# A two-layer graph network on one core: new order lists in a written-out program, maxima with turned sign, GpSimd's long instructions by graph

## The chip, the core and the metric

One core of one Trainium2 chip. The metric is the device time of one execution of the program in microseconds (us); lower is better. The engines are TensorE (PE; its weight loads are PEld), VectorE (DVE), ScalarE (ACT), GpSimd (POOL) and SyncE (SP), which here only issues DMAs. Each runs its own instruction stream, and they are ordered by semaphores alone.

## The reference

128 graphs of 128 nodes with 256 features, and an adjacency matrix each.

- **Layer 0** is a transformer block: layer norm; q, k, v (8 heads of 32); scores with `0.1 * adj` added where there is an edge and minus infinity elsewhere; softmax; product with v; output projection `wo` and residual; layer norm; `w1` (256 to 1024), gelu, `w2` (1024 to 256), residual.
- **Layer 1** has two rounds (C0 and C1 below), each: `q = x Wq + bq`, `k = x Wk + bk` (128 wide), scores divided by sqrt(128), masked softmax, `ctx = attn x`, `ctx Wc`, `x = layernorm(x + ctx) * g + b`.

```python
attn = jax.nn.softmax(scores, axis=-1)
x1 = residual + (out @ wo + bo)
mlp = jax.nn.gelu(n2 @ w1 + b1, approximate=False) @ w2 + b2
...
ctx = jnp.einsum('boi,bid->bod', attn, x)
ctx = jnp.einsum('bnd,ed->bne', ctx, Wc[k])
x = layer_norm(x + ctx, ln_g[k], ln_b[k])
```

## The kernel before, in words

**Tiling.** Four graphs form a group (NG = 32 groups). A group's rows are held as [128 nodes, 4 graphs, 256 features], its transposes as [128 features, 2 halves, 512 nodes]. f32 products are made of f16 parts: every operand is a high part (a cast, on ACT) and a low part (the rest, on DVE or POOL), and `mm3` (L243 to L247) issues high x high, high x low, low x high. So nearly each result of PE is read twice out of PSUM, by ACT for the high part and by DVE for the low part.

**Stages of a group.** `N`: load x (SP), statistics (DVE, L574 and L579), reciprocal root (POOL, `rsqrt`, L404 and L406), normalize (DVE `xh`, L587), transpose (PE `N.xT`), and `xb` adds the output bias on POOL (L441). `Q`: q0, q1, k0, k1 (halves of q and k; ACT L479, DVE L666), v0, v1. `stk`: SP copies q and k into the layout of the heads, 12 DMAs (L348). `A`, per graph b: `S` scores (PE L1041; DVE adds the mask, L680), `max` (DVE L685, and L687 turns the sign and scales into `nbias`), `exp` (ACT L490, one instruction a head), `PT` transposes (PE L1048; ACT L496, DVE L691), `AV` (PE; DVE L695, L699); then `oT`, `wo` (DVE L711), `st`, `xh`, and `x1b` on POOL (L437). `M`: `mT` (DVE L720), eight blocks `up` (PE, then gelu and cast on ACT, L510 and L513), `lo` (the low part, L252; even blocks DVE, odd ones POOL) and `down`; `x2` (DVE L728). `C0`, `C1`: `xT`, `q`, `k` (ACT L525), `S` (PE L1102, DVE L741), `max` (DVE L744, and L746 turns the sign of four numbers a partition), `ex` (ACT L532), `xW` (ACT L540), `cWb` (POOL L427, C1 only), `PT` (PE L1113, ACT L544), `PV` (PE L1122, DVE L763), `st`, `rs`, `xh`, and `af` (POOL L414 and L416: gain, then bias); `sto` stores the output.

**Order.** Five lists, one for each engine, give the steps of one iteration (`TENSOR`, `SCALAR`, `VECTOR`, `GPSIMD`, `SYNC`). The number behind a step says which group it treats: in iteration n, `A.S2-1` is the score step of graph 2 of group n - 1. So an iteration has every stage once, of groups n + 1 to n - 4. `run` (L266) writes out the first and last iterations and runs the rest in a hardware loop, two iterations to a turn; here PE's iterations -1 to 7 and 30 to 35 are written out and 8 to 29 looped. The waits are made by `need` (L222): "this semaphore has reached the count of group g"; in the loop the count is worked out in a register.

**What waits for what.** PSUM has eight banks: 0 and 1 for A (`psA`), 2 for q, k, v and AV, 3 for q, k, v and `up` (`psUp`), 4 and 5 for M, 6 and 7 for C and N. A step of PE can start when its operands are there and the last reader of its bank is done: PE's `Q.k1` waits for DVE's q1 (same bank), `C1.PT` for ACT's eviction of C1.xW, `up0` for DVE's low part of mT. `hid_h` and `hid_l` are rings of three blocks. `adj_in` is one buffer that both masks use (`mA` for A, `mC` for C). SP's list is in order too: a load whose wait isn't over holds back the store behind it. `C0.af` on POOL waits until the last output left `x3` (`st_out`).

## Time and profile before

| | |
|---|---|
| time of the runs | 2272.46 us, median of 3 (2272.21 to 2272.55) |
| profiled execution | time 2277.72 us, span 2275.9 us |
| busy share of the span | PE 89%, DVE 83%, ACT 69%, PEld 66%, POOL 37% |
| PE's granted clock | 0.970 of full over the span |
| DMA | 108.6 MB, mean 48 GB/s |

The span goes from the first to the last instruction of the profiled execution; the time has 1.8 us around it. A busy PE counts overlapping matmuls, so its pitch is read from where matmuls start. Iterations are told by PE's list: iteration 4 starts at 247.6 us, 8 at 505.4, 30 at 1946.8 and 32 at 2079.5.

### The profile page before, as it was taken

How to read it: one execution, taken by the hardware profiler on the slowest of the kernel's cores; microseconds unless marked ns; L12 is line 12 of the kernel's file. 1: busy time of each engine (PE TensorE's matmuls, PEld its weight loads, DVE VectorE, ACT ScalarE, POOL GpSimd, SP SyncE). 2: the span in 40 equal slices, each digit the busy share in tenths (PEclk: the TensorE clock that was granted, in tenths of full speed). 3: DMA queues.
4: the chain of work that ended last, by engine and by line, in shares of the span. 5: the costliest groups of instructions: out<-in, count | busy, mean ns of one | idle time of the engine just before them, and what ended most of it. 6: DMA issues, size and time to landing. Idle time of an engine off the chain costs nothing.

```text
span 2275.9 us, 47439 instructions
## 1 busy us (share of the span) xinstructions
PE 2026.2 (89%) x16984; PEld 1512.2 (66%) x16984; DVE 1887.3 (83%) x3589; ACT 1562.6 (69%) x2994; POOL 845.8 (37%) x632
## 2 busy tenths in 40 slices
...
DMA packets 103649, 108.61 MB, mean 48 GB/s; under 512 B 9824, under 2 KB 78432, under 8 KB 103456
## 3 DMA queue, kind: packets, MB, share of 16 engines
...
q0 software_dynamic: 544, 0.80, 0.2%
...
## 4 chain that ended last, share of the span: by engine, by line
PE 56%; DVE 21%; ACT 13%; issue 7%; POOL 1%; DMA 0%; SPq 0%; DVEq 0%; POOLq 0%; ACTq 0%
PE ps L245 13%; PE ps L247 13%; PE ps L246 13%; PE ps L824 5%; PE ps L1122 5%; PE ps L1048 3%; DVE hid_l L252 3%; DVE nmax L685 3%; ACT area L490 3%; DVE xh L587 2%; PE ps L1102 2%; DVE rot_l L720 2%; DVE qk L666 2%; DVE st L574 1%; ACT L490 1%
## 5 line engine op out<-in xcount | busy, mean ns | idle before, releaser
L252 POOL TENSOR_TENSOR hid_l<-area,hid_h 128x512 f16<-128x512 f32 x128 | 148.7, 1162 | 748.7 <-ACT hid_h L513 748.7
L490 ACT ACTIVATE area<-area,nbias 128x128 f32<-128x128 f32 x1024 | 313.5, 392 | 1.0 <-DVE nbias L687 0.2
L245 PE MATMUL ps<-w_h,hid_h 128*128 128x256 f16 x1024 | 279.0, 272 | 2.7 <-DVE hid_l L252 1.6
L247 PE MATMUL ps<-w_h,hid_l 128*128 128x256 f16 x1024 | 279.1, 273 | 0.0
L246 PE MATMUL ps<-w_l,hid_h 128*128 128x256 f16 x1024 | 279.1, 273 | 0.0
L510 ACT ACTIVATE area<-ps,b_col 128x512 f32<-128x512 f32 x256 | 176.1, 688 | 83.5 <-PE ps L247 82.4
L680 DVE TENSOR_TENSOR area<-ps,biasA 128x1024 f32<-128x1024 f32 x128 | 155.6, 1216 | 66.1 <-PE ps L1041 66.0
L245 PE MATMUL ps<-rot_h,w_h 128*128 128x512 f16 x512 | 195.0, 381 | 12.7 <-DVE rot_l L720 11.2
L246 PE MATMUL ps<-rot_l,w_h 128*128 128x512 f16 x512 | 194.7, 380 | 0.0
L247 PE MATMUL ps<-rot_h,w_l 128*128 128x512 f16 x512 | 194.7, 380 | 0.0
L404 POOL TENSOR_TENSOR ve<-mv,eps_cols 128x4 f32<-128x4 f32 x128 | 26.7, 209 | 418.4 <-DVE mv L579 417.5
L525 ACT ACTIVATE cq<-ps,cb_col 128x512 f32<-128x512 f32 x64 | 43.9, 686 | 192.1 <-PE ps L247 192.1
L245 PE MATMUL ps<-xT_h,wqk_h 128*128 128x512 f16 x256 | 100.0, 390 | 76.6 <-DVE qk L666 51.5
L513 ACT CAST hid_h<-area 128x512 f16<-128x512 f32 x256 | 158.3, 618 | 8.2
L691 DVE TENSOR_TENSOR pT<-ps,pT 128x1024 f16<-128x1024 f32 x128 | 155.3, 1214 | 5.4 <-ACT pT L496 5.4
L685 DVE TENSOR_REDUCE nmax<-area 128x8 f32<-128x1024 f32 x128 | 155.3, 1213 | 1.1
L824 PE MATMUL ps<-ident,area 128*128 128x128 f32 x1024 | 136.7, 277 | 21.9 <-DVE area L587 19.1
L252 DVE TENSOR_TENSOR hid_l<-area,hid_h 128x512 f16<-128x512 f32 x128 | 137.7, 1076 | 21.7 <-ACT hid_h L513 20.5
L416 POOL TENSOR_TENSOR x<-x,cb_row 128x1024 f32<-128x1024 f32 x64 | 153.7, 2401 | 5.0
L427 POOL TENSOR_TENSOR area<-area,cwb_row 128x1024 f32<-128x1024 f32 x32 | 75.3, 2352 | 199.8 <-ACT area L540 199.8
L1048 PE MATMUL ps<-ident,area 128*128 128x128 f32 x1024 | 138.5, 280 | 11.3 <-ACT area L490 7.0
L245 PE MATMUL ps<-cw_h,cT_h 128*128 128x256 f16 x512 | 141.0, 275 | 6.1 <-DVE cs L741 6.1
...
## 6 DMA issues: line engine op xcount, KB each, us to landing
...
area<-in_L_gnn_w SPq DMA_DIRECT2D x2, 1024.0 KB, 11.6
area<-in_L_gnn_Wc SPq DMA_DIRECT2D x2, 256.0 KB, 11.6
...
```

What stands on the lines that cost most here:

```text
L245: pe.matmul(dst, lh, rh, start=start, stop=False, **kw)
L246: pe.matmul(dst, lh, rl, start=False, stop=False, **kw)
L247: return pe.matmul(dst, ll, rh, start=False, stop=stop, **kw)
L252: eng.tensor_tensor(hid_l[:, c % RING, :], hidden[:, c % 2, :], hid_h[:, c % RING, :], ALU.subtract).then_inc(done, 1)
L490: last = act.activation(sc[:, b % 2, h], sc[:, b % 2, h], ACT.Exp, bias=nbias[:, b, h:h + 1], scale=1.0 / QK_SCALE)
L510: act.activation(hidden[:, b % 2, :], psUp, ACT.Gelu, bias=b1_col[:, b:b + 1], scale=1.0 / W_SCALE).then_inc(a_gelu, 1)
L513: act.copy(hid_h[:, b % RING, :], hidden[:, b % 2, :]).then_inc(a_hi, 1)
L680: dve.tensor_tensor(sc[:, b % 2], psA_heads, biasA[:, b].unsqueeze(1).broadcast_to([P, H, P]), ALU.add).then_inc(d_S, 1)
L685: dve.tensor_reduce(nmax[:, b, :], sc[:, b % 2], AX.X, ALU.max).then_inc(d_max, 1)
L691: dve.tensor_tensor(pT16[:, b % 2, 1], psA_heads, pT16[:, b % 2, 0], ALU.subtract)\
L824: last = pe.transpose(dst[:, c, b * P:(b + 1) * P], rows[:, b, c * P:(c + 1) * P], ident[:, :])
L1048: last = pe.transpose(psA_heads[:, h], sc[:, b % 2, h], ident[:, :])
```

## The change

- The five lists have a new order, and the program is written out: no loop, all waits on constants. PE's waits for free PSUM banks (`freed`, in place of the branches of `need`) name the last reader of the bank by group.
- `tensor_reduce(..., negate=True)` gives minus the maximum. The two instructions that turned the sign (L687, L746) go. The scale 1/QK_SCALE moves from `exp` and `nbias` into the scores' step (scalar_tensor_tensor in place of tensor_tensor, L680), and the factor 1024 of the probabilities from the exponent into the two evictions of `PT` (L496, L691).
- POOL's seven long instructions of an iteration (L414, L416 twice each, L427, L437, L441; 128x1024) become four each, one for each graph (128x256), with the semaphore on the last.
- The ring of feed-forward blocks has four places.

```diff
-P_SCALE = math.log(1024.0)
-RING = 3
+P_SCALE = 1024.0
+RING = 4
...
-TENSOR = ["Q.k0+0", "M.down2-2", "A.S2-1", "M.up4-2", "C0.q-3", "A.PT1-1", "M.down3-2", "M.up5-2",
-          "C0.k-3", "Q.q0+0", "M.up6-2", "C0.S-3", "M.down4-2", "A.S3-1", "C0.xW-3", "Q.q1+0",
-          "A.AV0-1", "A.PT2-1", "M.down5-2", "A.AV1-1", "Q.k1+0", "C0.PT-3", "A.PT3-1", "A.AV2-1",
-          "C1.xT-4", "M.up7-2", "A.AV3-1", "M.down6-2", "A.oT-1", "C0.PV-3", "M.down7-2", "A.wo-1",
-          "C1.q-4", "C1.k-4", "A.S0+0", "C1.S-4", "Q.v1+0", "C1.xW-4", "M.mT-1", "A.S1+0",
-          "C1.PT-4", "Q.v0+0", "M.up0-1", "C1.PV-4", "A.PT0+0", "M.up1-1", "N.xT+1", "M.down0-1",
-          "M.up2-1", "M.down1-1", "C0.xT-2", "M.up3-1"]
-SCALAR = ["C0.xT-3", "M.up3-2", "A.exp1-1", "M.up4-2", "C0.q-3", "Q.k0+0", "M.up5-2", "C0.k-3",
-          "A.PT1-1", "Q.q0+0", "M.up6-2", "A.exp2-1", "C0.ex-3", "Q.q1+0", "C0.xW-3", "A.PT2-1",
-          "A.exp3-1", "Q.k1+0", "C0.PT-3", "A.PT3-1", "C1.xT-4", "M.up7-2", "A.oT-1", "C1.q-4",
-          "C1.k-4", "Q.v1+0", "C1.ex-4", "C1.xW-4", "M.mT-1", "C1.PT-4", "A.exp0+0", "M.up0-1",
-          "Q.v0+0", "M.up1-1", "A.PT0+0", "N.xT+1", "M.up2-1"]
-VECTOR = ["A.PT1-1", "C0.S-3", "C0.max-3", "Q.q0+0", "A.S3-1", "A.max3-1", "A.AV0-1", "M.lo6-2",
-          "Q.q1+0", "A.PT2-1", "A.AV1-1", "Q.k1+0", "A.AV2-1", "A.PT3-1", "C1.xT-4", "A.AV3-1",
-          "Q.mA+0", "A.oT-1", "C0.PV-3", "M.x2-2", "A.wo-1", "A.st-1", "A.S0+0", "C1.S-4",
-          "C1.max-4", "A.xh-1", "A.max0+0", "N.st+1", "Q.v1+0", "M.mT-1", "A.S1+0", "N.xh+1",
-          "C1.PV-4", "M.lo0-1", "A.max1+0", "Q.v0+0", "M.mC-2", "N.xT+1", "A.PT0+0", "M.lo2-1",
-          "C1.st-4", "C0.xT-2", "A.S2+0", "C0.st-3", "C1.xh-4", "M.lo4-1", "Q.k0+1", "C0.xh-3",
-          "A.max2+0"]
-GPSIMD = ["M.lo1-1", "M.lo3-1", "N.xb+1", "C1.rs-4", "C0.rs-3", "M.lo5-1", "C1.af-4", "A.x1b-1",
-          "C0.af-3", "M.lo7-1", "A.rs+0", "C1.cWb-3", "N.rs+2"]
-SYNC = ["Q.ldA+0", "Q.stk+0", "N.ld+1", "M.ldC-2", "C1.sto-4"]
+TENSOR = ["A.S2-1", "M.up3-2", "M.down1-2", "C0.xT-3", "M.up4-2", "M.down3-2", "Q.k0+0", "A.PT1-1",
+          "M.down2-2", "M.up5-2", "C0.q-3", "Q.q0+0", "M.up6-2", "C0.k-3", "A.S3-1", "Q.q1+0",
+          "C0.S-3", "A.AV0-1", "M.down5-2", "A.PT2-1", "C0.xW-3", "M.down6-2", "Q.k1+0", "C0.PT-3",
+          "A.AV1-1", "A.PT3-1", "A.AV2-1", "C1.xT-4", "M.up7-2", "A.AV3-1", "M.down4-2", "A.oT-1",
+          "C0.PV-3", "M.down7-2", "A.wo-1", "C1.k-4", "C1.q-4", "A.S0+0", "C1.S-4", "Q.v1+0",
+          "C1.xW-4", "M.mT-1", "Q.v0+0", "A.S1+0", "C1.PT-4", "M.up0-1", "A.PT0+0", "C1.PV-4",
+          "M.up1-1", "M.down0-1", "M.up2-1", "N.xT+1"]
+SCALAR = ["A.exp1-1", "C0.xT-3", "M.up4-2", "Q.k0+0", "A.PT1-1", "M.up5-2", "C0.q-3", "Q.q0+0",
+          "M.up6-2", "C0.k-3", "A.exp2-1", "Q.q1+0", "C0.ex-3", "A.PT2-1", "C0.xW-3", "A.exp3-1",
+          "C0.PT-3", "Q.k1+0", "A.PT3-1", "C1.xT-4", "M.up7-2", "A.oT-1", "C1.k-4", "C1.q-4",
+          "Q.v1+0", "C1.ex-4", "M.mT-1", "C1.xW-4", "A.exp0+0", "C1.PT-4", "M.up0-1", "A.PT0+0",
+          "M.up1-1", "M.up2-1", "N.xT+1", "Q.v0+0", "M.up3-1"]
+VECTOR = ["Q.k1+0", "A.AV2-1", "A.PT3-1", "A.AV3-1", "C1.xT-4", "A.oT-1", "C0.PV-3", "M.x2-2",
+          "A.wo-1", "A.st-1", "A.S0+0", "C1.S-4", "C1.max-4", "A.xh-1", "A.max0+0", "N.st+1",
+          "Q.v1+0", "M.mT-1", "A.S1+0", "M.mC-2", "N.xh+1", "A.max1+0", "M.lo0-1", "C1.PV-4",
+          "A.PT0+0", "C1.st-4", "N.xT+1", "Q.v0+0", "C1.xh-4", "M.lo2-1", "A.S2+0", "C0.xT-2",
+          "A.max2+0", "Q.k0+1", "C0.st-3", "M.lo4-1", "A.PT1+0", "Q.q0+1", "A.S3+0", "C0.S-2",
+          "A.max3+0", "C0.max-2", "A.AV0+0", "M.lo6-1", "Q.q1+1", "Q.mA+1", "A.PT2+0", "C0.xh-3",
+          "A.AV1+0"]
+GPSIMD = ["M.lo7-2", "A.rs-1", "N.rs+1", "C1.cWb-4", "M.lo1-1", "C1.rs-4", "M.lo3-1", "C1.af-4",
+          "N.xb+1", "M.lo5-1", "A.x1b-1", "C0.rs-3", "C0.af-3"]
+SYNC = ["Q.stk-2", "N.ld-1", "Q.ldA-1", "M.ldC-3", "C1.sto-6"]
...
-            start, stop = (4 - min(aheads)) // 2, (NG - max(aheads)) // 2
-            for n in range(-max(aheads), 2 * start):
-                iteration(n // 2, n % 2)
-            with eng.Fori(start, stop) as it:
-                iteration(it, 0)
-                iteration(it, 1)
-            for n in range(2 * stop, NG - min(aheads)):
+            for n in range(-max(aheads), NG - min(aheads)):
                 iteration(n // 2, n % 2)
...
-            def over_graphs(row):
-                return row.unsqueeze(1).broadcast_to([P, B, D])
+            def by_graph(dst, src, row, op, signal):
+
+                for b in range(B):
+                    last = pool.tensor_tensor(dst[:, b], src[:, b], row, op)
+                last.then_inc(signal, 1)
 
             def affine(g, l, dst, src):
 
                 need(pool, d_xh[2 + l], g, 1, 1)
-                pool.tensor_tensor(dst, src, over_graphs(cg_row[:, l, :]), ALU.mult).then_inc(p_cg[l], 1)
+                by_graph(dst, src, cg_row[:, l, :], ALU.mult, p_cg[l])
                 need(pool, p_cg[l], g, 1, 1)
-                pool.tensor_tensor(dst, dst, over_graphs(cb_row[:, l, :]), ALU.add).then_inc(p_c[l], 1)
+                by_graph(dst, dst, cb_row[:, l, :], ALU.add, p_c[l])
...
-                                                  bias=nbias[:, b, h:h + 1], scale=1.0 / QK_SCALE)
+                                                  bias=nmax[:, b, h:h + 1])
...
-                        act.copy(pT16[:, b % 2, 0], psA_heads).then_inc(a_PT, 1)
+                        act.activation(pT16[:, b % 2, 0], psA_heads, ACT.Copy, scale=P_SCALE).then_inc(a_PT, 1)
...
-                        dve.tensor_tensor(sc[:, b % 2], psA_heads,
-                                          biasA[:, b].unsqueeze(1).broadcast_to([P, H, P]),
-                                          ALU.add).then_inc(d_S, 1)
+                        dve.scalar_tensor_tensor(sc[:, b % 2], psA_heads, 1.0 / QK_SCALE,
+                                                 biasA[:, b].unsqueeze(1).broadcast_to([P, H, P]),
+                                                 ALU.mult, ALU.add).then_inc(d_S, 1)
                     elif stage == "A" and what[:3] == "max":
                         need(dve, d_S, g, B, b + 1)
-                        dve.tensor_reduce(nmax[:, b, :], sc[:, b % 2], AX.X, ALU.max).then_inc(d_max, 1)
-                        need(dve, d_max, g, B, b + 1)
-                        dve.tensor_scalar(nbias[:, b, :], nmax[:, b, :], -1.0 / QK_SCALE, P_SCALE,
-                                          ALU.mult, ALU.add).then_inc(d_nb, 1)
+                        dve.tensor_reduce(nmax[:, b, :], sc[:, b % 2], AX.X, ALU.max, negate=True).then_inc(d_max, 1)
                     elif stage == "A" and what[:2] == "PT":
                         need(dve, a_PT, g, B, b + 1)
-                        dve.tensor_tensor(pT16[:, b % 2, 1], psA_heads, pT16[:, b % 2, 0], ALU.subtract)\
-                           .then_inc(d_PT, 1)
+                        dve.scalar_tensor_tensor(pT16[:, b % 2, 1], psA_heads, P_SCALE, pT16[:, b % 2, 0],
+                                                 ALU.mult, ALU.subtract).then_inc(d_PT, 1)
...
-                            dve.tensor_reduce(cneg[:, l], cs[:, l], AX.X, ALU.max).then_inc(d_cmax[l], 1)
-                            need(dve, d_cmax[l], g, 1, 1)
-                            dve.tensor_scalar(cmax[:, l], cneg[:, l], -1.0, None, ALU.mult).then_inc(d_cnb[l], 1)
+                            dve.tensor_reduce(cmax[:, l], cs[:, l], AX.X, ALU.max, negate=True).then_inc(d_cmax[l], 1)
...
+            def freed(g, *before):
+
+                pair, odd = g
+                for signal, behind, per, k in before:
+                    if not isinstance(pair, int):
+                        pe.wait_ge(signal, pair * (2 * per) + ((odd - behind) * per + k))
+                        return
+                    group = 2 * pair + odd - behind
+                    if 0 <= group < NG:
+                        pe.wait_ge(signal, group * per + k)
+                        return
+
...
-                    elif step == "C1.S":
-                        need(pe, a_cq[1], g, 1, 1)
-                        if isinstance(it, int):
-                            need(pe, d_cy[0], g, 1, 2)
-                            need(pe, d_xT, g, 1, 5)
...
+                    elif step == "C1.S":
+                        freed(g, (a_cq[1], 0, 1, 1))
...
```

The other branches of `freed` follow the same pattern.

## Rows read from the trace of the kernel before

**Rows 1.** The page, busy time, share of the span and instructions of each engine.

```profile
PE 2026.2 (89%) x16984; PEld 1512.2 (66%) x16984; DVE 1887.3 (83%) x3589; ACT 1562.6 (69%) x2994; POOL 845.8 (37%) x632
```

**Rows 2.** Windows: stretch and length, busy PE, PEld, DVE, ACT, POOL, PE clock, DMA.

```profile
0.00:247.60 247.60, 174.53 (x1353) 126.53 (x1354) 155.28 (x287) 127.86 (x237) 44.39 (x55) 0.88 0.24 65
247.60:505.40 257.80, 245.10 (x2114) 184.49 (x2113) 233.82 (x435) 193.98 (x372) 98.08 (x72) 1.00 0.18 47
505.40:1946.80 1441.40, 1352.43 (x11617) 1018.39 (x11616) 1284.83 (x2443) 1066.28 (x2046) 574.71 (x418) 1.00 0.19 49
...
2079.50:2276.00 196.50, 129.37 (x857) 89.70 (x855) 97.41 (x217) 78.24 (x154) 77.70 (x51) 0.85 0.05 17
```

**Rows 3.** Timeline of PE, 477 to 495 us: start, us, what [idle before].

```profile
477.74 0.27 PE L245 MATMUL ps<-wo_h,rot_h 128*128 128x256 f16 x1
...
480.36 0.38 PE L245 MATMUL ps<-cT_h,cqk_h 128*128 128x512 f16 x1
...
493.22 0.38 PE L245 MATMUL ps<-rot_h,w_h 128*128 128x512 f16 x1 [0.28 <-DVE rot_l L720]
...
494.51 0.81 PE L1122 MATMUL ps<-area,cs 128*128 128x256 f32 x3
```

**Rows 4.** Pieces of the critical chain: start us, us, what.

```profile
469.26 0.02 PE ps L245
...
469.83 0.03 PE ps L247
...
1017.71 1.73 PE ps L1122 x8
1019.44 0.87 PE ps L1048 x8
...
1044.37 0.89 PE ps L1102 x8
...
1046.57 0.45 PE ps L1041 x8
```

**Rows 5.** PE's waits (us, times, longest): 247.6 to 505.4 twice, 505.4 to 1946.8 once.

```profile
PE ps L245 <- DVE qk L666: 6.6, 4, 2.3
PE ps L1113 <- ACT area L540: 2.4, 4, 0.6
...
PE ps L245 <- issue: 19.4, 10, 2.2
```

**Rows 6.** Timelines of DVE and POOL, 450 to 481 us.

```profile
457.21 2.36 POOL L437 TENSOR_TENSOR area<-area,b_row 128x1024 f32<-128x1024 f32 x1
...
457.33 2.26 DVE L746 TENSOR_SCALAR cmax<-cneg 128x4 f32<-128x4 f32 x1
...
462.86 2.36 POOL L416 TENSOR_TENSOR x<-x,cb_row 128x1024 f32<-128x1024 f32 x1
...
463.32 2.44 DVE L252 TENSOR_TENSOR hid_l<-area,hid_h 128x512 f16<-128x512 f32 x1
...
480.89 1.23 DVE L711 SCALAR_TENSOR_TENSOR area<-ps,xin 128x1024 f32<-128x1024 f32 x1
```

**Rows 7.** Groups by line: shapes, count | busy us, mean ns | idle before.

```profile
L746 DVE TENSOR_SCALAR cmax<-cneg 128x4 f32<-128x4 f32 x64 | 60.1, 939 | 2.2
L687 DVE TENSOR_SCALAR nbias<-nmax 128x8 f32<-128x8 f32 x128 | 45.0, 351 | 4.4
L680 DVE TENSOR_TENSOR area<-ps,biasA 128x1024 f32<-128x1024 f32 x128 | 155.6, 1216 | 66.1 <-PE ps L1041 66.0
...
L441 POOL TENSOR_TENSOR xin<-xin,bo_row 128x1024 f32<-128x1024 f32 x32 | 75.3, 2355 | 3.3 <-DVE area L587 3.3
...
L404 POOL TENSOR_TENSOR ve<-mv,eps_cols 128x4 f32<-128x4 f32 x128 | 26.7, 209 | 418.4 <-DVE mv L579 417.5
```

**Rows 8.** The instructions of L746: shortest/median/longest ns, first and last start.

```profile
L746 DVE TENSOR_SCALAR cmax<-cneg x64: 169/171/2264, 202.7 to 2251.9; 128x4 f32<-128x4 f32 x64
```

**Rows 9.** Timeline of SP's DMA queue, the 12 copies of one group.

```profile
469.56 9.19 SPq L348 DMA_DIRECT2D qkS<-qk  x12
```

More of the change, by code:

```diff
@@ L153, in graph_blocks @@
         nmax = sb("nmax", [P, B, H])
-        nbias = sb("nbias", [P, B, H])
         rec = sb("rec", [P, B, H])
@@ L426, in iteration @@
                         need(pool, a_cW[1], g, 1, 1)
-                        pool.tensor_tensor(cW, cW, over_graphs(cwb_row[:, :]), ALU.add)\
-                            .then_inc(p_cW, 1)
+                        by_graph(cW, cW, cwb_row[:, :], ALU.add, p_cW)
                     elif stage == "C0" and what == "af":
@@ new lines, in iteration @@
+                    if step == "A.S2":
+                        freed(g, (d_PT, 0, 4, 1))
+                    elif step == "M.up3":
+                        freed(g, (a_gelu, 0, 8, 3))
+                    elif step == "C0.xT":
+                        freed(g, (d_xT, -3, 1, 1), (d_cy[1], 2, 1, 1), (d_cy[0], 1,
+                              1, 1))
+                    elif step == "M.up4":
+                        freed(g, (a_gelu, 0, 8, 4))
+                    elif step == "Q.k0":
+                        freed(g, (d_v[0], 1, 1, 1))
+                    elif step == "A.PT1":
+                        freed(g, (d_S, 0, 4, 3))
+                    elif step == "M.up5":
+                        freed(g, (a_gelu, 0, 8, 5))
+                    elif step == "C0.q":
+                        freed(g, (d_cT[0], 0, 1, 1))
+                    elif step == "Q.q0":
+                        freed(g, (d_qk[2], 0, 1, 1))
+                    elif step == "M.up6":
+                        freed(g, (a_gelu, 0, 8, 6))
+                    elif step == "C0.k":
+                        freed(g, (d_cT[0], 0, 1, 1))
+                    elif step == "A.S3":
+                        freed(g, (d_PT, 0, 4, 2))
+                    elif step == "Q.q1":
+                        freed(g, (a_gelu, 2, 8, 7), (d_v[1], 1, 1, 1))
+                    elif step == "C0.S":
+                        freed(g, (a_cq[0], 0, 1, 1))
+                    elif step == "A.AV0":
+                        freed(g, (d_qk[0], -1, 1, 1), (d_v[0], 0, 1, 1))
+                    elif step == "A.PT2":
+                        freed(g, (d_S, 0, 4, 4))
+                    elif step == "C0.xW":
+                        freed(g, (d_cS[0], 0, 1, 1))
+                        freed(g, (a_ck[0], 0, 1, 1))
+                    elif step == "Q.k1":
+                        freed(g, (d_qk[1], 0, 1, 1))
+                    elif step == "C0.PT":
+                        freed(g, (a_cW[0], 0, 1, 1))
+                    elif step == "A.AV1":
+                        freed(g, (d_o, 0, 4, 1))
```

198 lines of the change are left out of this document (43 added, 155 removed).

## The prediction

> **What bounds the kernel now.** I read the page first: TensorE (PE) is busy 89% of the span and VectorE (DVE) 83%, so either may set the time, and the shares don't say which [rows 1]. The stretches come next. Iterations 4 to 7 of the order list (each brings one group of four graphs through every stage) take 257.8 us, 64.5 each; iterations 8 to 29 take 1441.4 us, 65.5 each [rows 2]. The first four are written out already, the others run in the hardware loop. Written out alone is thus worth at most about a microsecond an iteration; the level of 65 has another cause.
>
> What PE must do in an iteration follows from counts in the code and the pitch at which its matmuls start at full clock [rows 3, 4]. Six matmuls of 512 columns take 1.29 us: 96 of them 20.7. The 24 of wo (256 columns) take 2.62: 192 of them 21.0. Eight transposes take 0.87: 80 of them 8.7. Eight score matmuls 0.45, four times: 1.8. C's f32 scores 0.89 and its last product 1.73, twice each: 5.2. 96 small AV matmuls, 23 of them in 0.57: 2.4. The sum is **59.8 us**. So some 4.7 to 5.7 us of every iteration is PE waiting, and the waits say for whom [rows 3, 5]:
> - 1.7 us on average and up to 2.3 before Q.k1, for DVE's q1 (it frees the PSUM bank).
> - 12.86 us pass between the end of wo (480.36) and the start of up0 (493.22), where PE has 10.9 us of work: 1.9 us are lost, 0.6 of them for C1.xW's eviction (C1.PT) and the last ones for DVE's mT (up0).
> - The rest, 0.7 us in the written stretch, is crumbs of 0.1 to 0.3 at S3, AV0 and PT2, and in the loop the jump back (below).
>
> Why is DVE late? Not by its arithmetic. The maximum's sign turn in C0.max, four numbers a partition, took 2.26 us, and GpSimd's (POOL) x1b was running from 457.21 to 459.57; DVE's lo6 (normally 0.68) took 2.44, until POOL's add of 2.36 was over [rows 6]. Over the run these sign turns take 0.94 us on average and 0.17 in the median, the nbias ones, as small, 0.35 on average [rows 7, 8]. DVE instructions with SBUF operands only are held until POOL's current instruction ends. So q1 stands behind lo6 behind a 2.36 us POOL instruction, and PE behind q1. That is what ends the longest wait.
>
> **The change, part by part.**
> (1) *Sign turned in the reduction.* Four nbias and two cmax instructions an iteration go. Without a hold each costs 0.17 and two semaphore hops: the reduction's end to the next start is 0.03 + 0.17 - 0.08 = 0.12, and becomes -0.08, so 0.2 saved each, 1.2 for six. With the holds in their means it is 6 x 0.2 + 4 x (0.35 - 0.17) + 2 x (0.94 - 0.17) = 3.5 us of DVE per iteration. That negating costs the reduction anything is not in the trace; bounds: nothing, or a second small instruction of 0.17 inside (which only gives back the 1.2). I take nothing. The scale moves into scalar_tensor_tensor instead of tensor_tensor; at 128x1024 from PSUM the one took 1.23 (L711), the other 1.22 [rows 6, 7], so eight of them cost under 0.1. The copy with a scale on ACT I take at the plain cast's price.
> (2) *POOL by graph.* Seven instructions of 2.36 an iteration become 28. A piece of 128x256 lies between a quarter, 0.59, and the line through 128x4 (0.209) and 128x1024 (2.355), 0.74 [rows 7]. I take 0.65: 2.6 instead of 2.36 a step, POOL stays under half busy. A hold on DVE is then at most 0.7 instead of 2.4. Whether DVE gets in between two pieces with no wait between them is not shown. In the trace it got in at the next boundary even where POOL's next instruction started at once, so I take that it does. If it does not, the long holds stay.
>  The Trainium skill says the same lock otherwise (SBUF — State Buffer, SBUF: two separate sides): the shared port pair goes to whoever starts first, for the whole instruction. By that rule too pieces shorten the hold. Its GPSIMD Engine Reference (3.1) speaks against pieces, since each instruction pays a software dispatch again; by the 0.74 bound, which has such a cost in it, this makes an af pair 5.9 instead of 4.7 us.
> (3) *Written out.* In the loop PE waits 19.4 us for nothing that the profile shows, ten times up to 2.2, at the list's end [rows 5]. This goes. The written stretch shows no new wait in its place. It is contained in the per-iteration sum below, since that starts from the floor.
> (4) *Order.* Q.k0 moves behind up3, down1, C0.xT, up4, down3; Q.q1 on DVE stands well before PE's Q.k1: PE reaches k1 25.9 us into its list, DVE can finish q1 at about 24. The wait of 1.7 to 2.2 us goes. Late next is Q.k1's own way: on ACT it stands behind exp3 and C0.PT, DVE ends it about 30.0 into the list. Behind it SP issues 12 copies in 9.2 us [rows 9], landed 2.3 later: 41.5, and S0 needs them at 42.9. Covered with 1.4 us. In SP's list the adjacency load for C waits for mA, which now ends late, and the store of the output is queued behind it; POOL's C0.af waits for that store. DVE has seven instructions (6.3 us) and some waits before C0.PV needs that af (5.2 us in pieces plus about 1 for the store). Covered, with 2 us.
>  Now the stretch wo to up0, zero at wo's end. DVE's order there is the old one, and each step takes its pitch in the timeline of before: wo to 1.4, st 3.4, S0 4.5, C1.S 5.1, C1.max 5.8, xh 7.1, max0 8.3, N.st 10.1, v1 10.7, mT 11.85, PE's up0 at **12.0** (before 12.86: 0.4 less by two removed instructions, 0.4 because DVE's wo started only at 480.89, behind x2 [rows 6]). ACT's side gives the same: mT is transposed at 9.3, ACT mT to 10.5, C1.xW to 11.5, C1.PT 11.6, up0 12.1. Against 10.9 that is a stall of 1.1. Then exp0 (11.5 to 13.95 on ACT) must precede PT0, which stands right behind up0 (13.4) instead of behind C1.PV: 0.7 us of new stall. C1.PV needs POOL's cWb, now queued behind N.rs: 0 to 0.5, I take 0.1. PT2 behind exp2 and other crumbs: 0.1 to 0.4, I take 0.2. Ring of four: up4 and later need a down less, which only gives cover; nothing.
>  Sum: 59.8 + 1.1 + 0.7 + 0.1 + 0.2 = **61.9 us** an iteration, bounds 60.4 (stretch well covered) and 63.5 (pieces at 0.74 and every crumb of before kept).
>
> **The sum**, against the profiled execution (span 2275.9, time 2277.7, median of the runs 5.3 lower). Iterations 4 to 31 stand between 247.6 and 2079.5 [rows 2]: 1831.9 us. 28 x 61.9 = 1733.2. Filling (247.6) and draining (196.4) are chains of one group with PE at 0.88 and 0.85 of its clock; fewer DVE steps give back a few us, POOL's pieces cost some: -6, between -15 and +8. Span 2275.9 - 98.7 - 6 = 2171.2; plus 1.8 outside, less 5.3: **2167.7**, say 2167.
>
> **Rivals.**
> - *PE at its floor* (60.5 or less). For it: DVE is busy 58.5 us an iteration (233.8 over four [rows 2]) and 3.5 of it go, and by my walk PE waits for it at wo to up0 alone. Against: exp0 before PT0. 28 x 60.4 with -6: 2126.
> - *The holds stay.* POOL's pieces are back to back, DVE doesn't get in, or each piece is dear; only the removed instructions and the order help. Half of the 5.1 us of waiting is kept, 63.5 to 65: 2212 to 2250.
> - *Slower, by C0.af.* Eight pieces in place of two, behind a store that is issued later, with 7.5 us or so until C0.PV(next) writes over their input and PE waits behind DVE. It costs nothing up to 0.9 us a piece; from there 8 us per us of piece. From 1.4 us a piece an iteration passes 65.5, at 1.6 it is 67 or 2315. For: nothing in the trace has this shape. Against: 0.74 by the nearest rows.
> - *The written-out program is fed too slowly*, so each engine pays at its list's end what PE pays now, and that eats the gain: about 2270. Against: iterations 4 to 7 [rows 2]. The Trainium skill (Runtime: NRT & Kernel Launch, Instruction fetch mechanics) has a taken branch break the sequential prefetch and straight code stream; the jump's gaps [rows 5] agree with that.
>
> **Chances.** Forecast, 2140 to 2205: 0.55. Floor: 0.22. Holds stay: 0.15. Slower: 0.05. Fed too slowly: 0.03. The range reaches into floor and holds: 2125 to 2212. Faster by over 0.2% (what a measurement of this kernel can tell from no change) 0.92, within it 0.03, slower 0.05.
>
> **What would show it.** Right: iterations of 61 to 63 us; no wait of PE for L666 before k1; DVE's lo and xh instructions with no maximum beyond 1.4 us; POOL pieces at 0.6 to 0.75; PE waits for mT (up0) and exp0 (PT0) of about a microsecond each; no wait of S0 for the copies. Wrong: DVE instructions held over several POOL pieces; S0 waiting for SP's copies; C0.PV waiting for POOL's af; new "issue" time on PE.

## The result and the profile after

The changed kernel takes **2195.8 us** (median of 4 runs, 2192.4 to 2197.2) against 2272.5 (2272.2 to 2278.5) for the kernel before, run beside it: a ratio of 0.9655, 95% interval 0.9641 to 0.9668. Run again later on another occasion it took 2196.6 (2195.9 to 2199.6), 0.9655 [0.9634, 0.9676]. Forecast were 2167, with 2125 to 2212 as the range. The time lies inside, 29 us above the point.

The profiled execution has a time of 2195.1 us, a span of 2193.1 and a mean granted clock of 0.971. Busy time, share of the span and instructions, from the page (compare [rows 1]):

```profile
PE 2016.2 (92%) x16984; PEld 1499.2 (68%) x16984; DVE 1721.4 (78%) x3397; ACT 1558.7 (71%) x2994; POOL 961.0 (44%) x1304
```

DVE lost 192 instructions and 166 us, POOL gained 672 and 115 us. PE's work is what it was.

Windows of the kernel after, cut at the same iterations as [rows 2] (0 to 4, 4 to 8, 8 to 30, and from 32 on):

```profile
0.00:242.70 242.70, 172.96 (x1326) 124.58 (x1327) 145.26 (x268) 124.45 (x233) 47.97 (x73) 0.87 0.25 66
242.70:491.70 249.00, 244.63 (x2114) 183.52 (x2113) 210.92 (x411) 193.38 (x373) 112.42 (x150) 1.00 0.19 50
491.70:1862.80 1371.10, 1345.30 (x11619) 1009.46 (x11617) 1176.64 (x2312) 1063.48 (x2047) 654.71 (x880) 1.00 0.20 52
...
1987.70:2194.00 206.30, 131.79 (x882) 90.97 (x882) 86.31 (x213) 81.30 (x158) 87.49 (x123) 0.84 0.04 15
```

The reader is to see three things. The middle iterations take 62.3 us (1371.1 / 22) and were 65.5. The fill is 4.9 us shorter. The drain (1987.7 to the span's end at 2193.1) is 205.4 us and was 196.4. The two lists begin with different steps, so these borders are not the same point of the work: taken at A.S2 in both kernels, the fill is 7.4 us shorter, the drain 10.3 longer, and the sum of the three parts is the same.

PE's longest waits in the middle stretch, 491.7 to 1862.8: total us, times, longest (compare [rows 5]):

```profile
PE ps L1026 <- ACT cq L518: 8.3, 22, 0.4
PE ps L1037 <- ACT area L533: 6.0, 22, 0.3
PE ps L972 <- ACT area L483: 5.1, 22, 0.2
PE ps L243 <- POOL hid_l L250: 3.0, 3, 1.2
```

The wait for DVE's q1 before Q.k1 is gone, and so is "issue". In the first three, PE waits each iteration for an eviction (C1.S, C1.PT) or an exp (PT0). The last line is new: down7 waits for POOL's lo7, in a few iterations only.

Are the holds gone? DVE's and POOL's groups of the whole run (mean ns behind the busy us; compare [rows 7]), and DVE's lo in 500 to 1850:

```profile
L678 DVE TENSOR_REDUCE nmax<-area 128x8 f32<-128x1024 f32 x128 | 154.8, 1210 | 0.2
...
L673 DVE SCALAR_TENSOR_TENSOR area<-ps,biasA 128x1024 f32<-128x1024 f32 x128 | 155.0, 1211 | 37.9 <-PE ps L965 37.9
```

```profile
L403 POOL TENSOR_TENSOR x<-x,cb_row 128x256 f32<-128x256 f32 x256 | 178.2, 728 | 5.0
...
L403 POOL TENSOR_TENSOR xin<-xin,bo_row 128x256 f32<-128x256 f32 x128 | 99.7, 812 | 3.7 <-DVE area L580 3.7
...
L403 POOL TENSOR_TENSOR x<-xh,cg_row 128x256 f32<-128x256 f32 x128 | 89.0, 728 | 295.7 <-DMA out<-x 272.6 <-DVE xh L580 23.1
```

```profile
L250 DVE TENSOR_TENSOR hid_l<-area,hid_h 128x512 f16<-128x512 f32 x86 | 60.1, 699 | 0.1
```

The reduction with `negate` takes 1.21 us, the scores' step as before 1.21. lo has a mean of 0.70 (0.68 in the median, 1.38 at most over the run), so it is hardly held. A POOL piece takes 0.73 us in the median of every line of code, where I took 0.65. The means of 0.77 to 0.81 come from single pieces of up to 1.22 us, and those are held by DVE. One such place, of DVE and POOL around 629 us:

```profile
628.47 0.74 POOL L403 TENSOR_TENSOR xin<-xin,bo_row 128x256 f32<-128x256 f32 x1
...
629.82 0.66 DVE L250 TENSOR_TENSOR hid_l<-area,hid_h 128x512 f16<-128x512 f32 x1
629.85 1.22 POOL L403 TENSOR_TENSOR xin<-xin,bo_row 128x256 f32<-128x256 f32 x1
```

DVE's lo starts just ahead of POOL's last piece, and the piece takes about 0.5 us more than the 0.74 of its like. So each of the two engines holds the other. And POOL waits 272.6 us in all for the output's store before it may write `x` (it was 39.1 us in the kernel before).

### The profile page after: what moved, and what is told of

Read it like the earlier page. It is cut to its first block, busy times and chain, and to the rows that moved or that the text cites. A ratio compares the mean times of both kernels' runs of the same rounds, so it can differ in the third digit from the quotient of the medians.

```text
span 2193.1 us, 45905 instructions
## 1 busy us (share of the span) xinstructions
PE 2016.2 (92%) x16984; PEld 1499.2 (68%) x16984; DVE 1721.4 (78%) x3397; ACT 1558.7 (71%) x2994; POOL 961.0 (44%) x1304
## 4 chain that ended last, share of the span: by engine, by line
PE 72%; ACT 13%; DVE 6%; POOL 4%; issue 3%; DMA 2%; SPq 1%; DVEq 0%; POOLq 0%; ACTq 0%
PE ps L243 18%; PE ps L245 17%; PE ps L244 17%; PE ps L812 5%; PE ps L972 5%; PE ps L1046 5%; ACT area L483 4%; PE ps L1026 3%; POOL x L403 3%; ACT cs L525 2%; DMA out<-x 2%; ACT area L533 2%; ACT L525 2%; PE ps L965 1%; ACT cq L518 1%
## 5 line engine op out<-in xcount | busy, mean ns | idle before, releaser
L483 ACT ACTIVATE area<-area,nmax 128x128 f32<-128x128 f32 x1024 | 312.5, 390 | 0.8
L403 POOL TENSOR_TENSOR x<-xh,cg_row 128x256 f32<-128x256 f32 x128 | 89.0, 728 | 295.7 <-DMA out<-x 272.6
L518 ACT ACTIVATE ck<-ps,cb_col 128x512 f32<-128x512 f32 x64 | 44.1, 689 | 199.0 <-PE ps L245 199.0
L673 DVE SCALAR_TENSOR_TENSOR area<-ps,biasA 128x1024 f32<-128x1024 f32 x128 | 155.0, 1211 | 37.9 <-PE ps L965 37.9
L403 POOL TENSOR_TENSOR x<-x,cb_row 128x256 f32<-128x256 f32 x256 | 178.2, 728 | 5.0
L681 DVE SCALAR_TENSOR_TENSOR pT<-ps,pT 128x1024 f16<-128x1024 f32 x128 | 155.7, 1216 | 3.2 <-ACT pT L489 3.2
L678 DVE TENSOR_REDUCE nmax<-area 128x8 f32<-128x1024 f32 x128 | 154.8, 1210 | 0.2
L972 PE MATMUL ps<-ident,area 128*128 128x128 f32 x1024 | 136.3, 276 | 16.4 <-ACT area L483 11.3
L972 PEld LDWEIGHTS ps<-ident,area 128*128 128x128 f32 x1024 | 113.0, 141 | 45.2 <-DVE area L673 22.8
L245 PE MATMUL ps<-cw_h,cT_l 128*128 128x256 f16 x512 | 139.6, 273 | 0.0
## 6 DMA issues: line engine op xcount, KB each, us to landing
area<-in_L_gnn_w SPq DMA_DIRECT2D x2, 1024.0 KB, 11.3
area<-in_L_gnn_Wc SPq DMA_DIRECT2D x2, 256.0 KB, 11.3
```

Of the source, the lines that this page charges most:

```text
L245: return pe.matmul(dst, ll, rh, start=False, stop=stop, **kw)
L403: last = pool.tensor_tensor(dst[:, b], src[:, b], row, op)
L483: last = act.activation(sc[:, b % 2, h], sc[:, b % 2, h], ACT.Exp, bias=nmax[:, b, h:h + 1])
L673: dve.scalar_tensor_tensor(sc[:, b % 2], psA_heads, 1.0 / QK_SCALE, biasA[:, b].unsqueeze(1).broadcast_to([P, H, P]), ALU.mult, ALU.add).t ...
L678: dve.tensor_reduce(nmax[:, b, :], sc[:, b % 2], AX.X, ALU.max, negate=True).then_inc(d_max, 1)
L681: dve.scalar_tensor_tensor(pT16[:, b % 2, 1], psA_heads, P_SCALE, pT16[:, b % 2, 0], ALU.mult, ALU.subtract).then_inc(d_PT, 1)
```

## The experiments

Each kernel was timed five or six times, beside runs of the kernel before. "Iteration" is the mean length of PE's iterations 5 to 28, and a step's wait is the mean of what lies between PE's starts beyond the pitch of the work between them. In the kernel after they are C1.S 0.54, C1.PT 0.43, PT0 0.39, up0 0.29, PT2 0.25 and down7 0.22: 2.1 of the 2.5 us between the 59.8 counted for PE's work and the 62.3 measured. The rest is spread in amounts of 0.05 and less and isn't told from the count of the work itself.

| | edit | median (range), us | ratio [95%] | iteration |
|---|---|---|---|---|
| after | | 2195.8 (2192.4 to 2197.2) | 0.9655 [0.9641, 0.9668] | 62.32 |
| e1 | after, POOL whole | 2182.6 (2178.8 to 2185.6) | 0.9596 [0.9582, 0.9610] | 62.08 |
| e2 | after, sign by its own instruction | 2225.1 (2223.2 to 2229.5) | 0.9787 [0.9773, 0.9800] | 63.35 |
| e3 | after, looped | 2224.1 (2219.5 to 2224.7) | 0.9760 [0.9746, 0.9774] | 63.34 |
| e4 | after, store ahead of ldC | 2185.1 (2183.5 to 2187.7) | 0.9604 [0.9591, 0.9617] | 62.10 |
| e5 | before, written out | 2266.2 (2259.8 to 2272.1) | 0.9952 [0.9934, 0.9970] | 65.13 |
| e6 | e5 + sign | 2187.6 (2185.6 to 2188.5) | 0.9605 [0.9592, 0.9617] | 62.44 |
| e7 | e5 + pieces | 2183.4 (2180.4 to 2185.8) | 0.9582 [0.9569, 0.9596] | 62.20 |
| e8 | e5 + sign + pieces | 2186.3 (2185.2 to 2187.7) | 0.9611 [0.9598, 0.9624] | 62.18 |
| e9 | after + e1 + e4 + other drain | 2179.5 (2172.4 to 2180.5) | 0.9578 [0.9557, 0.9600] | 62.03 |
| e10 | e9 + stretch reordered | 2368.3 (2360.4 to 2369.1) | 1.0397 [1.0370, 1.0423] | 68.83 |
| e12 | e10, cWb ahead of N.rs | 2224.9 (2224.7 to 2227.6) | 0.9772 [0.9759, 0.9785] | 63.67 |

(The kernel after, run again, is the eleventh; its time stands above.) Runs of one kernel differ by 2 to 12 us, largely together with their mean clock: e1 took 2178.8 at 0.975 and 2185.6 at 0.971. Differences of 2 or 3 us between two rows are therefore not read. The kernel before had medians of 2272.5 to 2277.5 us on the different occasions, so rows are best compared by their ratios. e4, e6 and e11 came out inside what was expected for them, e9 inside its rival; e5 and e12 came out between the two ranges given for them, and e1, e2, e3, e7, e8 and e10 outside both.

### e1: are the pieces needed in the new order?

```diff
-                for b in range(B):
-                    last = pool.tensor_tensor(dst[:, b], src[:, b], row, op)
-                last.then_inc(signal, 1)
+                whole = row.unsqueeze(1).broadcast_to([P, B, D])
+                pool.tensor_tensor(dst, src, whole, op).then_inc(signal, 1)
```

> The changed kernel with POOL's seven long instructions whole again (128x1024), all else as changed. Theory 'holds': a DVE instruction with SBUF operands only waits for the end of POOL's current instruction, so holds grow from at most 1.2 us to up to 2.4; they sit on N.xh, C1.xh, mC and lo, and the stretch wo to up0 and the q1 before k1 get longer: 0.3 to 0.9 us an iteration, time 2205 to 2225. Rival 'cover': in the new order DVE runs ahead of PE wherever a hold falls, and the pieces cost POOL 0.73 to 0.81 each instead of a quarter of 2.36 (0.59), so whole instructions give 2186 to 2197, the drain alone being some 2 us shorter.

Measured: 13 us faster than the kernel after. PE's waits keep their size (C1.S 0.54, C1.PT 0.43, PT0 0.40, up0 0.29); only down7's falls from 0.22 to 0.05. The pieces do shorten the holds (DVE's lo has a mean of 0.85 here, 0.70 with pieces), but in this order PE has no wait that the shorter holds take away. In the profiled executions the 28 iterations take 7.3 us less and the drain 8.7: what the pieces add to POOL's chain is what counts.

### e2: the sign turned by instructions of its own

```diff
-                        dve.tensor_reduce(nmax[:, b, :], sc[:, b % 2], AX.X, ALU.max, negate=True).then_inc(d_max, 1)
+                        dve.tensor_reduce(pmax[:, b, :], sc[:, b % 2], AX.X, ALU.max).then_inc(d_pm, 1)
+                        need(dve, d_pm, g, B, b + 1)
+                        dve.tensor_scalar(nmax[:, b, :], pmax[:, b, :], -1.0, None, ALU.mult).then_inc(d_max, 1)
```

(the same for C's maxima)

> The changed kernel with the sign of the maxima turned in an instruction of its own again (six more small DVE instructions an iteration, 0.17 us each when not held, in all 0.2 us with the hops). Theory 'DVE chain': two of them (C1.max, max0) lie on DVE's chain from wo to mT, which ends the wait of up0, so 0.2 to 0.4 us an iteration, and now and then a hold of up to 0.8: time 2202 to 2212. Rival 'cover': ACT's evictions in the same stretch (C1.q, C1.xW, exp0) end PE's waits, DVE's share is hidden: 2195 to 2199.

Measured: 29 us slower than the kernel after, 1.03 us an iteration. The six instructions cost PE more than I thought. PE's waits of e2, 600 to 1850:

```profile
PE ps L246 <- POOL hid_l L253: 13.7, 18, 2.5
PE ps L246 <- DVE rot_l L715: 9.8, 20, 0.8
...
PE ps L1053 <- POOL area L406: 5.1, 20, 0.3
```

down7 now waits 0.81 on average (0.22 in the kernel after), up0 0.71 (0.29) and C1.PV 0.42 (0.03). DVE has no slack left ahead of mT, and from wo to up0 it is 12.68 us, 0.4 more. down7 is late by the chain that e4 below breaks, and not by DVE's C0.xh: POOL's C0.af waits in every iteration for the output's store, and that is issued 0.4 us later because mA ends 0.4 us later. POOL's wait for it in e2, 491 to 1862 us:

```profile
POOL x L406 <- DMA out<-x: 234.4, 22, 12.5
```

down7's 0.59 us more are over half of the 1.03, so a good part of the 29 us is the price of the store's place in SP's list. How much stays with the store first was not run.

### e3: the loop in the new order

```diff
+            start, stop = (4 - min(aheads)) // 2, (NG - max(aheads)) // 2
-            for n in range(-max(aheads), NG - min(aheads)):
+            for n in range(-max(aheads), 2 * start):
                 iteration(n // 2, n % 2)
+            with eng.Fori(start, stop) as it:
+                iteration(it, 0)
+                iteration(it, 1)
+            for n in range(2 * stop, NG - min(aheads)):
+                iteration(n // 2, n % 2)
```

> The changed kernel with its middle iterations in the hardware loop again (two iterations a turn), all else as changed. Theory 'jump': every engine pays 1 to 2.2 us at the jump, once in two iterations, and in the new lists no slack is left on PE to hide it: 0.6 to 1.1 us an iteration over 22 iterations, 2209 to 2220. Rival: the jumps fall into waits that are there anyway, 2195 to 2202.

Measured: 28 us slower than the kernel after in the medians, 24 by the ratios (0.9760 and 0.9655); 1.0 us an iteration. PE's waits of e3, 600 to 1900:

```profile
PE ps L971 <- issue: 22.4, 10, 2.4
```

The jump takes PE 2.2 us a turn, as in the kernel before [rows 5], and all of it is lost: the list now begins with A.S2, and PE has no other wait there into which the jump could fall.

### e4: the store ahead of the adjacency load

```diff
-SYNC = ["Q.stk-2", "N.ld-1", "Q.ldA-1", "M.ldC-3", "C1.sto-6"]
+SYNC = ["Q.stk-2", "N.ld-1", "Q.ldA-1", "C1.sto-6", "M.ldC-3"]
```

> The changed kernel with SP's store of the output ahead of the load of the adjacency for C (it stood behind it, and that load waits for mA). Theory 'store queue': the store is then issued some 12 us earlier, POOL's C0.af no longer waits for it (8.5 to 10 us each now), lo7 is on time, and down7's wait (0.22 us an iteration on average, up to 1.39) goes; the jumps of 1 us in four iterations go too: 2184 to 2190. Rival: down7's wait has another cause (POOL's pieces before lo7), and nothing changes: 2194 to 2197.

Measured: 11 us faster than the kernel after; the two profiled executions lie 7.5 apart. Every iteration takes 62.1 and down7 never waits. In the kernel after, iterations 11, 14, 17 and 30 take 63.1 to 63.5. The chain that it breaks is this, in the kernel after (timelines of DVE, SP's queue, POOL and PE, 702 to 717 us: start, us, what, [idle before]):

```profile
702.86 0.69 DVE L638 SCALAR_TENSOR_TENSOR biasA<-biasA,adj_in 128x512 f32<-128x512 f32 x1
...
703.72 0.37 SPq L351 DMA_DIRECT2D adj_in<-in_adj  x1
704.21 0.43 SPq L355 DMA_DIRECT2D out<-x  x1
...
709.08 2.78 POOL L403 TENSOR_TENSOR x<-xh,cg_row 128x256 f32<-128x256 f32 x4 [10.84 <-DMA out<-x]
711.94 2.77 POOL L403 TENSOR_TENSOR x<-x,cb_row 128x256 f32<-128x256 f32 x4
714.67 1.16 POOL L250 TENSOR_TENSOR hid_l<-area,hid_h 128x512 f16<-128x512 f32 x1
...
715.88 0.28 PE L243 MATMUL ps<-w_h,hid_h 128*128 128x256 f16 x1 [0.80 <-POOL hid_l L250]
```

The last step of mA ends; the load for C that waited for it goes; half a microsecond behind it the store, whose data had long been ready. POOL's C0.af has waited 10.8 us for it, runs 5.6 us, then comes lo7, and down7 is 0.8 us late. POOL's waits of the two kernels in 491.7 to 1862.8, after first, then e4:

```profile
POOL x L403 <- DMA out<-x: 220.0, 22, 11.3
```

```profile
POOL x L403 <- DVE xh L580: 173.1, 22, 8.1
```

With the store first, POOL waits for DVE's C0.xh instead, and 47 us less.

### e5 to e8: the parts on the old order

e5 writes the kernel before out and changes nothing else. e6 adds the turned sign (with the scales moved as in the change), e7 the pieces, e8 both; lists and ring stay the old ones.

```diff
-            with eng.Fori(start, stop) as it:
-                iteration(it, 0)
-                iteration(it, 1)
-            for n in range(2 * stop, NG - min(aheads)):
+            for n in range(-max(aheads), NG - min(aheads)):
                 iteration(n // 2, n % 2)
```

> The kernel before, written out and nothing else. Iterations 4 to 7 (written out) took 64.5 us, 8 to 29 (looped) 65.5, so theory 'jump' gives 0.4 to 0.8 us for each of 22 iterations, 2255 to 2264. Rival 'fetch': straight code for all engines is fed more slowly than the loop and gives it back, 2270 or more.

> The kernel before, written out, with the sign turned in the reduction; POOL's instructions whole, old order. After e1 and e2, theory 'sign': the small sign-turning instructions were what was held longest (C0.max until the end of POOL's x1b, 2.26 us), and without them DVE reaches lo6 about 2 us earlier, so the wait before k1 nearly goes even with whole POOL instructions: 62.2 to 62.8 us an iteration, 2185 to 2203. Rival 'length': lo6 is still held behind C0.af's 2.36 us and q1 with it, so the wait before k1 stays at 1 us or more: 2215 to 2240.

> The kernel before, written out, with POOL's instructions by graph; sign turned separately as before, old order. Theory 'sign': shorter holds (0.7 instead of 2.3) give most of the k1 wait back too, but six small instructions stay: 62.8 to 63.6 us an iteration, 2205 to 2228. Rival 'pieces cost': POOL's pieces (0.73 to 0.81) delay its rs and lo steps and DVE is held again and again: 2235 to 2262.

> The kernel before, written out, with the turned sign and POOL's pieces, but its own order lists and ring of three: all of the change but the order. Theory 'holds first': the longest wait (Q.k1 for q1 behind a held lo6, 1.86 us an iteration) comes from the holds, so it falls below 0.4 without any new order, the loop's jump goes and wo to up0 loses 0.4: 63.0 to 63.8 us an iteration, time 2205 to 2225. Rival 'order first': the wait before k1 stays because q1 stands behind lo6 and max3 in DVE's list, 64.3 or more an iteration, 2240 to 2255.

Written out alone: 0.5% faster (0.3 to 0.7), 11 us against the kernel before beside it. The sign alone on top: 0.9605. The pieces alone on top: 0.9582. Both: 0.9611, so the second cure adds nothing to the first, and the old order with either is faster than the whole change (0.9655). PE's wait before Q.k1 (beyond pitch, an iteration) is 2.28 us in e5, 0.56 in e6, and none in e7 and e8. The waits of PE in 600 to 1850, of e5, e6 and e7:

```profile
PE ps L245 <- DVE qk L660: 40.2, 19, 2.3
PE ps L1107 <- ACT area L534: 11.5, 19, 0.6
PE ps L1096 <- ACT ck L519: 8.4, 20, 0.4
```

```profile
PE ps L1102 <- ACT area L534: 12.1, 20, 0.6
PE ps L1091 <- ACT ck L519: 8.4, 20, 0.4
PE ps L245 <- DVE qk L660: 8.1, 19, 1.0
```

```profile
PE ps L1108 <- ACT area L535: 12.6, 21, 0.6
PE ps L1097 <- ACT ck L520: 8.4, 20, 0.4
PE ps L245 <- DVE rot_l L715: 5.9, 20, 0.5
```

The DVE groups of the same three kernels in 500 to 1850 say why (mean ns behind the busy us):

```profile
L252 DVE TENSOR_TENSOR hid_l<-area,hid_h 128x512 f16<-128x512 f32 x83 | 93.8, 1131 | 3.2 <-ACT hid_h L507 2.3
...
L740 DVE TENSOR_SCALAR cmax<-cneg 128x4 f32<-128x4 f32 x41 | 50.8, 1239 | 1.4
```

```profile
L252 DVE TENSOR_TENSOR hid_l<-area,hid_h 128x512 f16<-128x512 f32 x86 | 84.9, 987 | 3.0 <-ACT hid_h L507 0.9
```

```profile
L252 DVE TENSOR_TENSOR hid_l<-area,hid_h 128x512 f16<-128x512 f32 x86 | 64.2, 746 | 0.0
...
L741 DVE TENSOR_SCALAR cmax<-cneg 128x4 f32<-128x4 f32 x44 | 11.2, 254 | 1.5
```

In e6 the instruction that was held (1.24 us, 0.17 unheld) is gone, though lo is still held to 0.99. In e7 it is there, and held only to 0.25. Either way q1 comes some 1.7 us or more earlier, and that is all PE asks. How DVE gets in between two pieces is seen in e7 (DVE and POOL, 702.7 to 704.6 us):

```profile
702.70 0.73 POOL L405 TENSOR_TENSOR x<-xh,cg_row 128x256 f32<-128x256 f32 x1 [0.47 <-DMA out<-x]
...
702.92 1.06 DVE L252 TENSOR_TENSOR hid_l<-area,hid_h 128x512 f16<-128x512 f32 x1
703.39 1.17 POOL L405 TENSOR_TENSOR x<-xh,cg_row 128x256 f32<-128x256 f32 x1
```

lo is held by the first piece and takes 0.4 us more than its 0.68. It ends at 703.98. The second piece starts at 703.39, without a gap, and takes 1.17 instead of 0.73: now POOL is the one that is held.

What neither cure touches is the stretch from wo to up0. It has a mean of 12.87 us in e5, 12.85 in e6, 12.86 in e7 and 12.85 in e8, as before the change (12.89). In the new order it is 12.68 with the sign instructions (e2) and 12.27 without. So in the old order something else than DVE's small instructions ends these waits; PE's list names ACT's eviction of C1.xW as the larger of them, and the new order puts that eviction behind mT's in ACT's list. What the new order wins there, 0.6 us an iteration, it pays with the new waits of PT0 (0.39) and PT2 (0.25): without the store's wait it takes 62.10 (e4), the old order 62.18 (e8).

### e9 to e12: on from the best, and two misses

e9 joins e1 and e4 and gives the iterations that only drain lists of their own: C0.st and C0.xh right behind C0.PV on DVE, C0.rs first on POOL.

```diff
+LATE = {VECTOR[0]: moved(VECTOR, ("C0.st-3", "C0.xh-3"), "C0.PV-3"),
+        GPSIMD[0]: moved(GPSIMD, ("C0.rs-3",), None)}
...
+            if isinstance(it, int) and 2 * it + odd >= NG + 1:
+                order = LATE.get(order[0], order)
```

> The changed kernel with POOL's instructions whole, the store ahead of the load of the adjacency for C, and other lists in the last three iterations only: DVE does C0.st and C0.xh right behind C0.PV, POOL does C0.rs first (in the drain they stood behind C1.PV, C1.st, C1.xh and C1.af of the group before, which are one long chain there). Level 62.0 us an iteration as with whole instructions. Theory 'drain order': the last C1.xT no longer waits for C0.xh (15.2 us of wait now), the drain shrinks from 205 to 185 to 192 us: 2160 to 2172. Rival: the drain is bound by its own chain of one group, and only the two known gains join, 2176 to 2184.

e10 then tries the stretch from wo to up0: v1 ahead of C1.S on PE, ACT's xW ahead of mT, and on DVE the following, so that mT comes sooner.

```diff
-          "C1.max-4", "A.xh-1", "A.max0+0", "N.st+1", "Q.v1+0", "M.mT-1", "A.S1+0", "M.mC-2",
-          "N.xh+1", "A.max1+0", "M.lo0-1", "C1.PV-4", "A.PT0+0", "C1.st-4", ...
+          "C1.max-4", "A.xh-1", "A.max0+0", "Q.v1+0", "M.mT-1", "A.S1+0", "N.st+1", "M.lo0-1",
+          "N.xh+1", "C1.PV-4", "A.PT0+0", "M.mC-2", "A.max1+0", "C1.st-4", ...
```

> e9 with the stretch from wo to up0 rearranged: PE does v1 before C1.S (so cq is out by then), ACT does C1.xW's eviction before mT (so C1.PT doesn't wait), DVE does N.st behind mT and S1, and PT0, mC and max1 after C1.PV. By the pitches of the trace the waits of C1.S (0.54), C1.PT (0.43), up0 (0.29) and PT0 (0.39) shrink to one of about 0.5 for mT, with 0.2 to 0.5 new at N.xT or S2: 61.0 to 61.5 us an iteration, 2135 to 2158. Rival: the later N.st holds up N.rs, N.xh and N.xT by more than is won: 62.0 or more, 2162 to 2180.

e12 is e10 with the one step moved that had broken it:

```diff
-GPSIMD = ["M.lo7-2", "A.rs-1", "N.rs+1", "C1.cWb-4", "M.lo1-1", ...
+GPSIMD = ["M.lo7-2", "A.rs-1", "C1.cWb-4", "N.rs+1", "M.lo1-1", ...
```

> e10 with one swap in POOL's list: C1.cWb ahead of N.rs. In e10 N.rs waited for the moved N.st, cWb stood behind it, and PE's C1.PV waited 4.95 us an iteration for cWb. Theory 'queue': with the swap that wait goes, and most of the 1.64 behind it (DVE's C1.PV late); what stays is C1.xW's wait for C1.S's eviction (0.95, v1 no longer stands between them) and up0: 62.0 to 63.0 us an iteration, 2165 to 2205. Rival: the moved N.st itself is late for N.xh and N.xT, and the wait only moves to N.xT: 64 or more, 2230 and up.

> The changed kernel once more, unchanged, beside the two above and the same runs of the kernel before, to anchor the small differences: ratio 0.964 to 0.967, 2190 to 2200. If it came out at 0.962 or less, the finding that the new order costs some 9 us against the old one (e8) would fall.

e9 is the fastest that was run, but with e1 and e7 inside its interval. Its drain is 194.7 us; e1's, without the other lists, was 196.7. What iteration 34 gained (56 to 44 us) iteration 33 gave back (44 to 54). e10 is slower than the kernel before. Timelines of POOL and PE around 992 us in e10:

```profile
991.80 0.20 POOL L409 TENSOR_TENSOR ve<-mv,eps_cols 128x4 f32<-128x4 f32 x1 [10.40 <-DVE mv L584]
...
993.05 2.82 POOL L416 TENSOR_TENSOR area<-area,cwb_row 128x1024 f32<-128x1024 f32 x1
...
996.01 3.41 PE L1058 MATMUL ps<-area,cs 128*128 128x256 f32 x8 [4.79 <-POOL area L416]
...
1039.28 1.89 PE L1058 MATMUL ps<-area,cs 128*128 128x256 f32 x8
```

The moved N.st lets POOL's N.rs wait, cWb is queued behind N.rs, and C1.PV loses 4.8 us an iteration. The iteration is 6.8 us longer than e9's, though. Most of the other 2 us is the clock. PE's granted clock falls to the lower of its two levels (1.2 and not 2.4 GHz) after that wait, and the same eight matmuls take 3.41 us here and 1.89 at 1039, where PE came to them without a wait. Windows of e10, from 997 to 999 us and from 1000 to 1004:

```profile
997.00:999.00 2.00, 2.00 (x6) 1.48 (x5) 0.24 (x2) 0.00 (x0) 0.00 (x0) 0.50 0.04 8
1000.00:1004.00 4.00, 4.00 (x29) 2.72 (x28) 4.00 (x8) 1.70 (x3) 1.25 (x1) 1.00 0.02 5
```

The same happens in each of e10's iterations, and the mean clock of 600 to 1900 us is 0.97 there, while it is 1.00 in e9 and e12. The expectation of e12 had put this second part down to DVE. With cWb first that wait is gone and the clock stays full (e12), yet the iteration is 63.67 us, still above the 62.03 of e9. PE's waits of e12, 600 to 1500:

```profile
PE ps L824 <- DVE xT_l L666: 16.5, 14, 1.2
PE ps L254 <- DVE cs L743: 11.0, 14, 0.8
```

The steps that were made later on DVE are missed at C0.xT, and C1.xW waits for C1.S's result now that v1 doesn't stand between.

## Why the prediction came out as it did

**Right.** Why PE waited: a long POOL instruction holds DVE, DVE's q1 is late, PE stands before Q.k1. e6 and e7 each take one link out, and the wait goes (to 0.56 and to nothing). DVE does get in between pieces that stand back to back, and its lo and xh instructions stay below 1.4 us. Written out is worth little in the old order (e5: 0.5%; the issue time was 19.4 us). No new issue time came up, S0 never waited for the copies, and PE's remaining waits stand where the walk through the lists put them: from wo to up0 it is 12.27 us (719.82 to 732.09; forecast 12.0), PT0 0.39 (0.7), C1.PV 0.03 (0.1). The 0.4 us that I gave the two removed instructions in that stretch is there in the new order (12.68 to 12.27, e2 and after) and not in the old one (12.87 to 12.85, e5 and e6).

**Too wide.** "DVE instructions with SBUF operands only are held" is more than the trace of before shows. The 128 reductions of L685 read and write SBUF and take 1.205 to 1.221 us, never held. What was held are instructions with one input that only scale or shift (tensor_scalar, up to 2.49 us for an xh of 0.41) and those with two different inputs in SBUF (lo, up to 2.85 in e5). The instructions that the change counts on are of these two kinds, so nothing of the sum changes.

**Mis-sized, by the steps of the sum.** From 2167 to 2196 are 29 us:
- *Iteration*, +11.8 us: 28 took 1745.0 instead of 1733.2, 62.3 each instead of 61.9. down7 is 0.22 of it. I had written "Covered, with 2 us" and about 1 us for the store. POOL waited 9.7 us each time (272.6 / 28) and up to 11.3. I had seen the queue on SP and didn't follow it in time: when mA ends, and how long the store takes to land behind it. e4 shows its price, 11 us in the medians. The other terms: the stretch lost 1.37 us (12.27 less 10.9) instead of 1.1, PT0 0.39 instead of 0.7, and the rest (PT2, C1.PV and crumbs) 0.54 instead of 0.3.
- *Edges*, +10.1: I forecast 6 us less than before and got 4 more. The fill gave 4.9 back as thought. The drain cost 9.0 more. There PE waits once for DVE's xh of the last C0 round, 15.2 us; before it was 12.7. This comes from the lists more than from the pieces: it is 14.3 in e1 and 10.2 in e7 and e8. A chain of one group pays every piece in full: 5.6 us for an af that took 4.75. In e8 (old lists, pieces) the drain is 198.6 and in e1 (new lists, whole) 196.7, so neither alone costs the 9 us, only the two together.
- *Median against profile*, +6 or so: I subtracted 5.3 because the median lay that far below the profiled execution of before. After, it lies 0.7 above. One profiled execution is a draw out of runs that spread by some microseconds with the clock; carrying its distance over was a mistake.
- *Pieces*: 0.73 us in the median, where I took 0.65 and gave 0.74 as the upper bound. The bound, a line through two other sizes, holds. What I left out is that the hold works the other way too: a piece that starts during a DVE instruction takes up to 1.22 us.
- *The rival "the holds stay"*: I priced it at 2212 to 2250, with half of PE's waiting kept if only the removed instructions and the order helped. e1 is that case, with whole POOL instructions, and takes 2182.6. The pieces were not needed for the time that I forecast.

The waits of the last group in the drain (1987 to 2194 of after):

```profile
PE ps L812 <- DVE xh L580: 15.2, 1, 15.2
PE ps L1046 <- POOL area L403: 8.0, 4, 2.3
```

**What I had not seen.** I built the sum from PE's floor and never asked which part brings what. They are cures of one wait. The turned sign takes away the instruction that is held, the pieces shorten the hold, and the order moves the reader away (the order without the other two was not run). On the old order the first or the second alone brings all there is, and I had expected 2205 to 2225 of e8. What is left after either is a level of 62.0 to 62.4 that every good variant shares. In the new order with whole POOL instructions (e1) nothing is gained over the old order with the sign (e6): 0.9596 and 0.9605, with overlapping intervals. With the pieces it is worse by about 10 us (after against e8), by the store's queue and the drain. (These pairs differ in the lists and in the ring of four; the ring was not run by itself.) That the time fell inside the range is therefore no proof of the order's part. What the new order asks in return is that nothing on DVE or PE slips: the six small instructions cost 29 us there (e2), of which I had counted 1.2 us of DVE an iteration and none of PE, and the jump 24 to 28 (e3). In the old order the same sign instructions beside the pieces cost nothing that can be told (e7 against e8), and the jump about 11 (7 to 15 by the interval of e5). There the jump's 0.88 us an iteration takes 0.42 off the wait before Q.k1, which is 1.86 in the kernel before and 2.28 in e5.

**Left open.** Whether the level of 62 can be brought to PE's 59.8: the tries at its largest stretch (e10, e12) moved the waits and did not remove them. And how much of the drain's 9 us is clock: from 1987.7 to 2120 the clock of the kernel after is 0.93, in the same part of e1 it is 0.97. The clock isn't all of it. Taken at A.S2, the drain of e7 (old lists, pieces) is 193.0 us at a clock of 0.84, and that of the kernel after 205.4 at 0.85; the five profiles with new lists and pieces lie at 203.0 to 207.8.
